# Attention score stacks built through DRAM, one 512-column score matmul per unit, and layers written out as a table of segments

## What is computed

```python
x = x + L0_xattn(layernorm(x), ctx, ctx, mask)            # A: masked attention, then W and b
x = x + L0_ffn(layernorm(x), weight)                      # Hadamard, 4-bit activations, ternary weights
x = x + L1_xattn(layernorm(x), ctx, bias)                 # C: attention with a bias per head, then an FFN
x = x + L1_ffn(layernorm(x))                              # 8 experts, each takes its best 512 tokens
# L0_xattn
scores = einsum('bhqd,bhkd->bhqk', q, k) / 4; scores = where(mask == 0, -1e9, scores)
out = einsum('bhqk,bhkd->bhqd', softmax(scores), v) @ W.T + b
# L1_xattn
q, k, v = x_q @ Wq.T, x_kv @ Wk.T, x_kv @ Wv.T
scores = einsum('bhqd,bhkd->bhqk', q, k) / 4 + bias
x = x_q + softmax_times_v @ Wo.T
x = x + gelu(layer_norm(x, g1, be1) @ W1.T + b1) @ W2.T + b2
return layer_norm(x, g2, be2)
```

## Time and profile before

| | us |
|---|---|
| median of 3 runs | 1176.57 |
| lowest and highest of the runs | 1172.53, 1179.02 |
| span of the profiled execution, first to last instruction | 1184.8 |
| of it until the first exponential | 24.4 |
| A0 to C7, first exponential to the end of the last units | 841 |
| rest of batch 7 up to the router's softmax | 50.9 |
| routing and experts | 268.4 |

### The profile page before, as it was taken

One profiled execution on the slowest core, in us unless ns is written; L12 is line 12 of the kernel. 1 busy time (PEld: TensorE's weight loads), 2 busy tenths in 40 slices (PEclk: granted clock), 3 DMA queues, 4 the chain that ended last, 5 costly groups with the idle time before them and its releaser, 6 DMA issues. The chain is left out here.

```text
span 1184.8 us, 21611 instructions
## 1 busy us (share of the span) xinstructions
PE 982.9 (83%) x6889; PEld 800.1 (68%) x6889; DVE 709.0 (60%) x2101; ACT 662.4 (56%) x1337; POOL 439.0 (37%) x625
## 2 busy tenths in 40 slices
PE   4897799897998989899888998877964329999996
PEld 3686577676776767777766786665743218889985
DVE  3666478585567758666765885652621755666442
ACT  2565467754675685576558577543531005776663
POOL 3312334151334326133422623322211124777762
PEclk9998579986897899698789989877777558999998
DMA  5900023023003202300320220220000403455542
GB/s 179 304 2 1 10 83 97 2 90 107 0 0 125 70 0 89 107 0 0 125 71 0 89 81 1 81 81 1 19 1 20 139 18 95 124 129 135 144 80 27
DMA packets 70976, 80.75 MB, mean 68 GB/s; under 512 B 3312, under 2 KB 67312, under 8 KB 70896
## 3 DMA queue, kind: packets, MB, share of 16 engines
q1 hardware_dynamic: 64752, 71.43, 18.6%
q0 software_dynamic: 6144, 8.39, 4.0%
HBM read 71.43 MB, written 8.39 MB: 67 GB/s over the span
## 5 line engine op out<-in xcount | busy, mean ns | idle before, releaser
L729 ACT ACTIVATE probs<-neg,neg_max 128x256 f32<-128x256 f32 x512 | 231.9, 504 | 57.4 <-DVE neg_max L592 57.0
L600 DVE TENSOR_TENSOR p_lo<-ps_t,p_hi 128x512 f16<-128x512 f32 x256 | 176.3, 689 | 120.7 <-ACT p_hi L737 119.3
L737 ACT ACTIVATE p_hi<-ps_t 128x512 f16<-128x512 f32 x256 | 150.8, 589 | 136.3 <-PE ps_t L376 135.9
L376 PE MATMUL ps_t<-ident,probs 128*128 128x128 f32 x1024 | 200.3, 327 | 6.2 <-ACT probs L729 5.4
L376 PEld LDWEIGHTS ps_t<-ident,probs 128*128 128x128 f32 x1024 | 128.3, 161 | 47.2 <-issue 13.3
L592 DVE CUSTOM_DVE_ANT_0 neg<-ps_s,bias_t 128x256 f32<-128x256 f32 x256 | 97.7, 419 | 59.3 <-PE ps_s L365 29.9
L925 POOL TENSOR_TENSOR o_sum<-o_raw 128x128 f32<-128x128 f32 x64 | 29.9, 467 | 271.2 <-ACT o_raw L821 271.2
L592 DVE CUSTOM_DVE_ANT_0 neg<-ps_s,mask_add 128x256 f32<-128x256 f32 x224 | 85.5, 419 | 60.9 <-issue 36.4
L347 PE MATMUL ps_m<-part_h,select 32*128 32x256 f32 x256 | 79.1, 369 | 44.1 <-DVE part_l L606 18.2
L347 PEld LDWEIGHTS ps_m<-part_h,select 32*128 32x128 f32 x256 | 49.6, 215 | 60.1 <-issue 37.8
L365 PE MATMUL ps_s<-k_stack_C,q_stack_C 64*128 64x256 f32 x288 | 83.0, 378 | 7.2 <-DVE neg_max L592 5.9
(11 more groups left out here) (244 smaller groups left out, 2337.5 us busy)
## 6 DMA issues: line engine op xcount, KB each, us to landing
bias_t<-in_bias SPq DMA_DIRECT2D x16, 2048.0 KB, 8.4
w1e<-in_w1e SPq DMA_DIRECT2D x8, 1024.0 KB
w2e<-in_w2e SPq DMA_DIRECT2D x8, 1024.0 KB, 6.1
ctxT_A<-in_ctxT SPq DMA_DIRECT2D x8, 256.0 KB, 8.2
mask_int<-in_mask SPq DMA_DIRECT2D x8, 256.0 KB, 7.8
v_raw_A<-in_ctx SPq DMA_DIRECT2D x8, 256.0 KB, 7.9
w<-in_w SPq DMA_DIRECT2D x2, 1024.0 KB, 8.9
ctxT_C<-in_ctxT SPq DMA_DIRECT2D x8, 256.0 KB, 2.7
```

The lines of the kernel that those rows point to most:

```text
L376: ins = nc.tensor.matmul(ps_t[u % 2][:, (i * QT + kb) * P:(i * QT + kb + 1) * P], probs[:, u % 2, i, kb * P:(kb + 1) * P], ident[:, :], st ...
L600: nc.vector.tensor_tensor(p_lo[:, u % 4, :], ps_t[u % 2][:, :], p_hi[:, u % 4, :], ALU.subtract).then_inc(lo_ready, 1)
L729: ins = nc.scalar.activation(probs[:, u % 2, i, :], neg[:, u % 4, i, :], ACT.Exp, bias=neg_max[:, u % 4, i:i + 1], scale=-1.0)
L737: nc.scalar.activation(p_hi[:, u % 4, :], ps_t[u % 2][:, :], ACT.Copy).then_inc(hi_ready, 1)
```

## The change

**Stacks.** `select` and `pe_stack` go, and with them their copies. High and low part stand in one tile, `part`. SP writes it to a DRAM tensor in four DMAs (`sp_part_out`, 512 KB) and reads it back: q with two DMAs into both halves of a tile of 128 rows (`sp_q_in`, 1 MB), k with four DMAs, each half row block repeated, into `k_diag` (`sp_k_in`, 1 MB). `k_diag` has 128 rows and two blocks of 256 columns per pair of heads, the rows of the other head being zero. It is zeroed once. One matmul with 128 rows and 512 columns gives the scores of both heads.

```diff
-            for i, h in enumerate(unit_heads(u)):
-                c, j = divmod(h // 2, 4)
-                r = slice(4 * DK * (h % 2), 4 * DK * (h % 2 + 1))
-                ins = nc.tensor.matmul(ps_s[u % 2][:, i * SEQ:(i + 1) * SEQ],
-                                       q_stack[buffers(seg.kind, seg.b)][r, c, j, qt * P:(qt + 1) * P],
-                                       k_stack[buffers(seg.kind, seg.b)][r, c, j, :], start=True, stop=True)
-            ins.then_inc(scores_ready, 1)
+            if u == 0:
+                pe.wait_ge(ld[f"q{i % 2}"], 32 * (i // 2 + 1))
+                pe.wait_ge(ld[f"k{i % 2}"], 64 * (i // 2 + 1))
+            wait(pe, neg_ready, g - 1)
+            nc.tensor.matmul(ps_s[g % 2][:, :], q_stack[i % 2][:, pair, qt * P:(qt + 1) * P],
+                             k_diag[i % 2][:, :, pair, :], start=True, stop=True).then_inc(scores_ready, 1)
...
+        def ac_part_high(ac, n, src, scale):
+            wait(ac, S["part_out"], 64 * n)
+            nc.scalar.activation(part_flat(0), src, ACT.Copy, scale=scale).then_inc(S["part_h"], 1)
...
+        def sp_part_out(sp, n, dram):
+            sp.wait_ge(S["part_l"], n + 1)
+            for j in range(4):
+                sp.dma_start(dram.rearrange("(pf s) (c j q) -> j pf s c q", s=2, c=DC, j=4)[j],
+                             part[32 * j:32 * j + 32, :, :, :].bitcast(F32)).then_inc(S["part_out"], 16)
+
+        def sp_q_in(sp, i, n):
+            sp.wait_ge(S["part_out"], 64 * (n + 1))
+            wait(sp, scores_ready, UNITS * (i - 1))
+            for copy in range(2):
+                sp.dma_start(q_stack[i % 2][QROWS * copy:QROWS * (copy + 1), :, :].rearrange("p g q -> p (g q)").bitcast(F32),
+                             q_dram[i % 2]).then_inc(ld[f"q{i % 2}"], 16)
```

**Order of the segments.** `layers`, `seg_a`, `seg_c`, `walk` and the `side` functions go. A table takes their place, and each engine's function is unrolled over it from i = -1 (preparation of A0) to NSEG + 2:

```diff
+SEGMENTS = [(A, 0), (A, 1)] + [s for b in range(2, NB) for s in ((A, b), (C, b - 2))] + [(C, NB - 2), (C, NB - 1)]
+KV = {POS[C, b] - 2: b for b in range(NB)}
+PREP_C = {POS[C, b] - 1: b for b in range(NB)}
+PREP_A = {POS[A, b] - 1: b for b in range(NB)}
+REST_A = {POS[A, b] + 1: b for b in range(NB)}
+FF1 = {POS[C, b] + 1: b for b in range(NB)}
+FF2 = {POS[C, b] + 2: b for b in range(NB)}
+FF3 = {POS[C, b] + 3: b for b in range(NB)}
+def ff1_slots(i):
...
+        pieces = {9: (0, 1), 10: (2,), 11: (3,), 12: (4,), 13: (5,), 14: (6,), 15: (7,)}
+        raw = (10, 12)
```

More of the change, by code:

```diff
@@ new lines, with prep_a_slots, prep_c_slots, rest_a_slots @@
+PART = part_numbers()
+def prep_a_slots(i):
+    return dict(k=0 if i < 0 else 6, stats=0, apply=1, bias=15 if i < 0 else 2, q=3, mask=8, values=3)
+def prep_c_slots(i):
+    if i in FF2 and i in REST_A:
+        return dict(stats=1, apply=2, T=3, q=(4, 5), parts=5, values=4, bank="m0")
+    return dict(stats=2, apply=3, T=5, q=(6, 7), parts=7, values=4, bank="m0" if i in REST_A else "m1")
+def rest_a_slots(i):
+    return dict(oT=4, out=(5, 6), x1=7, apply=8, T=9, had=(10, 11), amax=12, cap=13, qT=14, tern=15)
@@ L75, in wait, with ff3_slots @@
+def ff3_slots(i):
+    return dict(stats=0, apply=1, T=2, logits=3, copy=3, bank="s0" if i >= NSEG else "m1")
 def wait(eng, sem, value):
[L77 removed]
+    if value > 0:
         eng.wait_ge(sem, value)
@@ L173, in build @@
         nrm["R"] = nrm_r
[L175 to L185, removed]
+        w_b, w_b_pos, w_b_negv, w_b_tern = (hidT[:, 2 * n:2 * n + 2, :] for n in range(4))
+        w_b_bc = nrm["G"][:, :, 0:P]
         layer_memory.close()
@@ L980, in walk @@
-        def walk(main, prev, ahead, nxt, unit_first, unit_slot, tail, half_work, side):
-            for s in range(UNITS):
-                if main is not None:
-                    if s == 0 and not ahead:
-                        unit_first(main)
-                    unit_slot(main, s, nxt, prev if s < LAG else None)
-                elif s == 0 and prev is not None:
-                    tail(prev)
-                h = halves(s, main, prev)
-                if h is not None:
-                    half_work(*h)
-                side(s)
@@ new lines, in ac_exp, with ac_high_part @@
+        def ac_exp(ac, g):
+            ac.wait_ge(neg_ready, g + 1)
+            wait(ac, pt_ready, g - 1)
+            for j in range(2):
+                ins = nc.scalar.activation(probs[:, g % 2, j, :], neg[:, g % 3, j, :], ACT.Exp,
+                                           bias=neg_max[:, g % 3, j:j + 1], scale=-1.0)
+            ins.then_inc(exp_ready, 1)
+        def ac_high_part(ac, g):
+            ac.wait_ge(pt_ready, g + 1)
+            wait(ac, pv_done, g - 2)
+            nc.scalar.activation(p_hi[:, g % 3, :], ps_t[g % 2][:, :], ACT.Copy).then_inc(hi_ready, 1)
```

1559 lines of the change are left out of this document (815 added, 744 removed).

## The result

The changed kernel takes **1024.1 us** (median of 4 executions, 1022.7 to 1028.2) against 1177.8 for the kernel before in the same session: a ratio of **0.869, 95% interval 0.864 to 0.873**. That is faster, and inside the range of the prediction; the predicted 1040 was 16 us too long. The profiled execution has a span of 1020.9 us, 163.9 less than before.

What follows compares the result with a forecast made beforehand. The prediction took PE work in the slots as the bound, with two empty stretches and the Gelu groups added. Its nine terms summed to -136 us, a span of 1049 and a median of 1040 us, range 970 to 1115.

Steps and rivals of the forecast that it cites:

- Term 1: Score matmul: one 512-column matmul replaces the 64-row pair, saving 0.20 us per unit, four fifths on the path; -40 us.
- Rival D: Score matmul: the 512-column form costs PE as much as the pair; 1080 us, chance 0.06.
- Term 2: Stack steps: 112 steps at 0.55 us leave PE, four fifths on the path, copies costed at nothing; -50 us.
- term 8: New waits: ACT's high part waits for the previous part's store, +12 us; point 8 also held that loads stay hidden.
- term 4: Gelu: fewer groups between units, with k's and v's projections filling PE's idle time beside them; -25 us.
- term 3: Two empty stretches before C0 and C7: 68 us go, moved work puts 18 back on the path; -50 us.
- Term 5: FFN work in halves that fit a slot, so DVE and ACT run dry less; -10 us.
- Terms 6 and 7: Opening, with parts going out to DRAM and back, +10 us; end, with batch 6's FFN work moved there, +7 us.
- Rival B: The way through DRAM is late, each of 16 segments starting 5 us late, +80; 1120 us, chance 0.11.
- Term 9: Clock: PE does less per slot, so a lower granted clock was allowed for; +10 us.
- Rival C: The lighter PE is granted half clock in the layers, making the kernel slower; about 1265 us, chance 0.03.
- Rival A: PE stops being the bound and DVE and ACT keep pace; 970 us, chance 0.15.

Runs made afterwards that it cites:

- e5: Changed kernel with e1, e3 and e4 in one, so the new order and DRAM loads with the old engine work; 1199.2 us, ratio to the kernel before 1.012.
- e12: e5 with its seven groups of 32-row matmuls per segment in units 1, 3, ... 13 instead of 1 to 7; 1181.1 us, ratio to kernel before 0.996.
- e1: Changed kernel with each unit's score matmul made again of two 256-column matmuls on 64 rows; 1100.6 us, +76.5 against the changed kernel.
- e2: Changed kernel with the 512-column score matmul cut into two of 256 columns, both on 128 rows; 1023.9 us, -0.2 against the changed kernel.
- e3: Changed kernel with four 32-row matmuls put ahead of the scores of seven units per segment (112 groups); 1124.1 us, +100.0 against the changed kernel.
- e4: Changed kernel with the stack steps' copies again, 64 on ACT and 64 on DVE, into a spare tile; 1048.6 us, +24.5 against the changed kernel.
- e8: Changed kernel with the part tile doubled, so ACT's high part waits for the store two parts earlier; 1001.3 us, -22.8 against the changed kernel.
- e6: Changed kernel with the third FFN quarter copied raw as well, freeing the banks for k's and v's projections; 1006.4 us, -17.7 against the changed kernel.
- e9: Changed kernel with e6 and e8 in one; 992.5 us, ratio to the kernel before 0.837.
- e7: Changed kernel with the first two FFN quarters put through Gelu in slot 12 instead of copied raw; 1044.6 us, +20.5 against the changed kernel.
- e11: Changed kernel with q's stack read twice from DRAM, the second read waiting for the first; 1116.8 us, +92.7 against the changed kernel.

## Why the prediction was right, and where it was not

The total came out (-136 forecast, -164 measured in the spans, -154 in the medians), but out of a wrong split, and its closeness is luck. Terms 1 and 2 had 90 us for the work taken off the engines, where e5 and e12 put 175 and 157 on it. Terms 3 to 8 had 56 us for the order and the loads, where the same runs give between a gain of 5 and a loss of 15. The two errors went opposite ways. That the removed work pays for the change is what was right.

- **Term 1, scores, -40: measured -77 (e1, undone alone).** Mechanism right, size wrong. The rate of 0.20 us was read from the first score matmul's start on the earlier trace rows and missed what the 64-row pair costs ahead of that start; it is 0.29 at the full clock (0.20 behind the values). The run paid 0.30 for each unit, at a mean clock of 0.83 against 0.89, so the four fifths were too low as well, or the slower clock made up for them. The Trainium skill, TensorEngine Tiling (Array Packing), Key Properties, says that a change of tiling mode drains TensorE. e1 and e2 agree: +76.5 us with 64-row tiles, none with as many matmuls on 128 rows. Rival D is out.
- **Term 2, stack steps, -50: measured -100 for PE (e3), -24.5 for the copies (e4).** I took 0.55 us where a row said 0.67, and again four fifths; among 128-row work it is 0.86. Beside the old pair a step is cheaper, so the 100 is not what the steps cost in the kernel before: all three kinds of work together are 175 (e5), not the 201 of e1, e3 and e4. The copies were costed at nothing with the remark that they come back, up to 38 us, should PE no longer lead; by e4 they do.
- **Terms 3, 4, 5 and 8, the order.** Prediction, terms 3 to 8: -56. Measured with the old PE work in place, by the ratios to the kernel before: between +15 (e5) and -5 us (e12). The 68 us of the empty stretches did go. But the order gives back: ACT's wait for the single part tile, **22.8** (e8) where term 8 had 12; k's and v's projections behind the Gelus instead of beside them, **17.7** (e6, 9 of it seen in these slots), where term 4 counted this as a gain; the moved work, 18 by term 3; the opening, 6; the end, 6. That sums to 71, or to 62 with the 31.6 that e9 gives for the first two together. Against it stand the 68 us and the merged Gelu's 20.5 (e7). What is left of that gain isn't seen in e12, and I can't say where it went; one lead is the clock of all units, 0.82 in e5 against 0.86 before. The experiments measure the order on top of the old work, and the PE work on top of the new order. What the order is worth once PE is light was not tried.
- **Term 4's failing step** is the sentence that the projections of k and v "now lie in the same slot as the group in most of these, where PE would be idle". They lie in the slot, but both write banks that hold FFN quarters until Gelu has read them.
- **Term 5, -10:** at most 6, not shown.
- **Terms 6 and 7:** +6.1 and +6.1 against +10 and +7.
- **Term 8, its other half:** "about 20 us against 10 for the way out and back" was wrong on both sides. C3's stack is due two slots before the segment, at slot 14, 14.7 us after the part, and the way takes 13.5 us. Point 8 didn't price k's way, which was late for A1 and A3, by 5.7 us together. Rival B's 80 us did not happen, but they were one read of 6 us away (e11), not 10 us.
- **Term 9, clock, +10: the sign was wrong.** The mean of all units rose from 0.86 to 0.89, about 0.01 of it, by an estimate from the earlier trace rows, because the two stretches at 0.79 and 0.74 are gone; in the steady segments it hardly moved (0.88 and 0.87 before, 0.86 in A5 and 0.88 in C3). It is 0.83 in e1 and in e3, 0.82 in e5, and 0.91 in e6 and e9. The Trainium skill, TensorE: Matmul & The Clock Gate, Part 1, says that the throttled clock is the default and activity releases it; I had drawn from it that a lighter PE would be slowed. In these runs taking 64-row and 32-row work away went with a higher clock, and putting it back with a lower one, though PE was busier then. More waits lowered it too, to 0.85 in e11 with PE busy for 72% of the units' time. So it isn't a smaller busy share alone that sets the mean, and why it rose is not shown further. Rival C is out.
- **Rival A, PE no longer the bound,** came true in part: e4 shows that ACT and DVE cost time now, and PE is busy for 79% of the units' time instead of 88%. But e1 and e3 show that PE work added still costs about its whole length.
- **The range.** The root of the squared half widths of the nine bounds is 61 us, not some 45, which fits only the bounds on the faster side. The stated range of 970 to 1115 is wide enough for either.
- **Signs named ahead.** Right: no empty stretch, no `select` work, A segments near 40 (33 to 41), end of the units (697 against 725, earlier still). Wrong: score spacing 0.23 read at the scores' start (0.42, for the reason in e2), PE's busy time -120 (-206), C segments near 46 (five of them 48.7 to 50.4, over the 48 that was set as the mark of being wrong; C0 41 and C6 39), slot with Gelu near 7 (8.9 to 10.3), ACT's wait for the part over 2 us a segment, which said beforehand that term 8 was too small.

## What to carry to other kernels

Price a matmul form from the start of the instruction ahead of it to the start of the one behind it: what a tile of fewer rows costs lies partly ahead of its own record. Work that is moved "into an idle slot" overlaps only if its PSUM bank is free then; look up who holds the bank. When a data path leaves the engines for DRAM, count its slack in slots at the new, shorter slot length, and double the small tile that it starts from: here that tile alone was worth 2%.

## What the runs showed of the hardware

Two 256-column matmuls on 128 rows cost the same as one of 512 columns (1023.9 against 1024.1 us for the whole kernel with 256 such units; 0.452 against 0.449 us from the matmul ahead to the transposes behind). The same two on 64 rows cost 0.29 us more between a 256-column matmul and transposes on 128 rows, 0.20 behind the values, 0.43 at half clock; a group of four on 32 rows costs 0.86, 0.77 and 1.45. A part (high and low, 512 KB) is stored to DRAM and read back twice over in 13.5 us, from the start of ACT's write to the landing of the later read (C3); 2.5 of it are SP's issue of four DMAs.
